# Layer 0 of a four-layer graph network: one wide first product on VectorE, and the destination's rows gathered from DRAM by GpSimd instead of selected by a one-hot product on TensorE

## The reference, cut to what matters

```
msg_s, msg_v = table_src[src] + table_dst[dst]        # 64 scalars, 32 vectors; tables = normed rows @ weights
w1 = rbf @ W_rbf                                      # 224 weights an edge, from 16 features
m1_s, m1_v = cg_tp(msg_s, msg_v, y0, y1, w1)          # first product
a = leaky(m1_s @ W_alpha) . alpha_dot                 # 4 logits an edge
alpha = softmax of a over the edges of one dst
val_s, val_v = m1 @ Ws_val, Wv_val, gated by sigmoids
m2_s, m2_v = cg_tp(val_s, val_v, y0, y1, w2)          # second product
agg[dst] += alpha * (m2 @ W_vlin)                     # 4 heads of 40

cg_tp(s, v, y0, y1, w): scalars  w_ss*s*y0, w_vv0*(v.y1)/sqrt3
                        vectors  w_sv*s*y1, w_vs*v*y0, w_vv1*cross(v, y1)/sqrt2
```

## Time and profile before

| | |
|---|---|
| median of 3 runs | 12166.53 us |
| the profiled execution, its own time | 12098.74 us |
| its span, first to last instruction | 12096.9 us |
| busy: PE, DVE, ACT, POOL | 9397.7, 9136.3, 7003.3, 6367.4 us |
| granted clock of TensorE, mean | 0.897 |
| layer 0's loop over pairs | about 1590 to 6550 us of the span |

### The profile page before, as it was taken

One profiled execution on the slowest core, in us unless ns is written; L12 is line 12 of the kernel. 1 busy time (PEld: TensorE's weight loads), 2 busy tenths in 40 slices (PEclk: granted clock), 3 DMA queues, 4 the chain that ended last, 5 costly groups with the idle time before them and its releaser, 6 DMA issues. The chain is left out here.

```text
span 12096.9 us, 245491 instructions
## 1 busy us (share of the span) xinstructions
PE 9397.7 (78%) x46500; PEld 6592.8 (55%) x46501; DVE 9136.3 (76%) x32454; ACT 7003.3 (58%) x26255; POOL 6367.4 (53%) x9502
## 2 busy tenths in 40 slices
PE   4421188888888888888888788887788888788887
PEld 1211177777777777777777344445433335444445
DVE  6702078888888888888887899995565555899996
ACT  0000067777777777777776555553566666676764
POOL 0677646666666666666542455551355553455551
PEclk9855589999999999999998999996799999999997
DMA  6433211111111111111111343333222223343333
GB/s 262 53 66 70 64 31 31 30 30 30 30 31 30 31 30 30 31 30 31 27 17 38 82 87 86 87 85 46 43 53 52 52 52 54 84 87 85 86 85 60
DMA packets 1798441, 691.91 MB, mean 57 GB/s; under 512 B 1586190, under 2 KB 1677258, under 8 KB 1798346
## 3 DMA queue, kind: packets, MB, share of 16 engines
q0 software_dynamic: 219136, 411.56, 14.6%
q1 hardware_dynamic: 1572154, 275.26, 13.5%
q10 hardware_dynamic: 7056, 4.02, 0.1%
HBM read 514.24 MB, written 171.77 MB: 57 GB/s over the span
## 5 line engine op out<-in xcount | busy, mean ns | idle before, releaser
L963 POOL DMA_INDIRECT shared<-table,rec x2640 | 2560.4, 970 | 2508.8 <-issue 1058.4
L1045 PE MATMUL bank<-tp,oh 128*128 128x480 f32 (+1 forms) x5280 | 2407.3, 552 | 6.3 <-DVE tp L1122 4.6
L997 ACT ACTIVATE tp<-tp,rec 128x64 f32<-128x64 f32 x7920 | 2030.3, 335 | 234.1 <-DVE tp L1093 153.2
L1037 PE MATMUL bank<-w_fc,hT 128*128 128x448 f32 x2640 | 1368.5, 601 | 701.5 <-ACT hT L981 447.9
L1680 ACT ACTIVATE shared<-bank 128x512 f32<-128x512 f32 x1760 | 973.6, 595 | 961.9 <-PE bank L1755 955.1
L1045 PEld LDWEIGHTS bank<-tp,oh 128*128 128x128 f32 x5280 | 921.0, 195 | 856.8 <-issue 843.5
L1755 PE MATMUL bank<-ident,tp 128*128 128x128 f32 x7040 | 1054.0, 299 | 265.5 <-ACT tp L813 218.2
L1093 DVE TENSOR_TENSOR tp<-bank,shared 128x256 f32<-128x256 f32 x1320 | 560.2, 424 | 924.3 <-PE bank L1045 613.4
L782 POOL DMA_INDIRECT rec_dst<-ACC x784 | 813.5, 1038 | 602.5 <-issue 571.9
L1755 PEld LDWEIGHTS bank<-ident,tp 128*128 128x128 f32 x7040 | 889.9, 154 | 303.3 <-ACT tp L813 253.6
L1644 POOL DMA_INDIRECT gat<-table,rec x880 | 866.7, 985 | 277.0 <-issue 190.7
(11 more groups left out here) (248 smaller groups left out, 22541.0 us busy)
## 6 DMA issues: line engine op xcount, KB each, us to landing
shared<-table,rec POOLq DMA_INDIRECT x2640
rec_dst<-tp SPq DMA_DIRECT2D x44, 900.0 KB, 23.6
ACC<-in_attrs SPq DMA_DIRECT2D x56, 623.0 KB
rec_src<-tp SPq DMA_DIRECT2D x44, 730.0 KB, 19.9
efr<-rec_src SPq DMA_DIRECT2D x440, 64.0 KB
efr<-rec_dst SPq DMA_DIRECT2D x440, 64.0 KB
ACC<-in_attrs SPq DMA_DIRECT2D x196, 130.0 KB
rec<-rec_dst SPq DMA_DIRECT2D x1320, 10.0 KB
```

What stands on the lines that cost most here:

```text
L963: nc.gpsimd.indirect_dma_start(out=gatx[:, u, g, 0:L.row], out_offset=None, in_=tables[L.n][:, :], in_offset=IOff(ap=rec[:, u, g, L.idx:L. ...
L997: done = nc.scalar.activation(t[:, g, lo:lo + 64], t[:, g, 0:64], ACT.Copy, scale=rec[:, u, g, L.y + k:L.y + k + 1])
L1037: nc.tensor.matmul(pW[u % 2][:, 0:448], hT[:, u % 2, :], fc2[:, :], start=True, stop=True)\
L1045: done = nc.tensor.matmul(pS[u % 2][:, 0:TW], oh[:, u, g, :], tp[:, u % 2, g, 64:64 + TW], start=g == 0, stop=g == G - 1)
```

## The change

The destination's rows are stored to a DRAM table of their own, `table_d`, in the node work at the start (49 more DMAs of 80 KB on ACT's queue), and in the loop POOL gathers them by destination into `gat_d`: two more indirect DMAs a pair. The two matmuls of L1816 and PE's register load go. The record gets one more integer (90 to 91 floats), the destination. The first product becomes the wide form of `edge_loop`: ACT scales 96 of each group's weight columns by y0 in PSUM (two instructions), DVE makes the product, POOL no longer takes part. `message` becomes two instructions, with the first vector's column block written twice. Further: the write of the new maximum to `M` is moved from `maxima` to behind `weigh` (`held`); `gates` becomes one instruction for both groups; `weigh` becomes one instruction of 328 columns, since `pH` gets a column of ones for each head; DVE keeps one of its two block numbers in three steps of four. ACT makes the scalar part of the first product ahead of its copies of stage a, not behind them.

```diff
             def rows_out(b):
...
+                if b >= 1:
+                    dst_rows_out(b - 1)
+            def dst_rows_out(b):
+                ac.wait_ge(first_td_kept.h, first_td_kept.at(b + 1))
+                ac.dma_start(table_d[b * P:b * P + P, :], first_TD[:, b, :]).then_inc(first_dst_stored.h, 16)
...
POOL     gather(a):
+                            nc.gpsimd.indirect_dma_start(
+                                out=gat_d[:, s4, g, :], out_offset=None, in_=table_d[:, :],
+                                in_offset=IOff(ap=rec[:, s4, g, 2:3].bitcast(i32), axis=0))
...
POOL     step:
-                        if b:
-                            part(*b, msg[:, b[1] % 2], msg_ready, tp1_ready, 0, pooled1)
                         if a:
                             gather(*a)
                         if c:
-                            part(*c, vsv[:, c[1] % 2], gated, tp2_ready, 1, pooled2)
+                            part(*c)
...
ACT      step:
+                        if b:
+                            ac.wait_ge(sv1_ready.h, sv1_ready.done(*b))
+                            product_scalar(*b, tp[:, 0, :, 0:64], tp[:, 0, :, 64:544], L).then_inc(axes1.h, 1)
                         if a: (copies of efT and ohT)
-                        if b:
-                            ac.wait_ge(sv1_ready.h, sv1_ready.done(*b))
-                            product_scalar(*b, t_sv, 0, L).then_inc(axes1.h, 1)
...
                             product_scalar(*c, ...)
+                        if a:
+                            ac.wait_ge(w_ready.h, w_ready.done(*a))
+                            for g in range(G):
+                                y0w = pW[:, 224 * g + 64:224 * g + 160]
+                                last = nc.scalar.activation(y0w, y0w, ACT.Copy, scale=rec[:, a[1] % 4, g, L.y0:L.y0 + 1])
+                            last.then_inc(w_scaled.h, 1)
...
PE       step:
                         if a:
-                            row = block_of(pe, *a)
                             pe.wait_ge(copied.h, copied.done(*a))
-                            pe.wait_ge(msg_ready.h, msg_ready.free(*a, 1))
-                            for g in range(G):
-                                last = nc.tensor.matmul(pB[:, F * g:F * g + F], ohT[:, s4, g, :],
-                                                        flat(TD[:, row, :]), start=True, stop=True)
-                            last.then_inc(dst_ready.h, 1)
...
DVE      message:
-                        nc.vector.tensor_tensor(msg[:, u % 2], gat[:, u % 4], pB[:, 0:320]...)
+                        nc.vector.tensor_tensor(rows[:, u % 2, :, 0:F], gat[:, u % 4], gat_d[:, u % 4], ALU.add)
+                        nc.vector.tensor_tensor(rows[:, u % 2, :, F:F + 64], gat[:, u % 4, :, 64:128],
+                                                gat_d[:, u % 4, :, 64:128], ALU.add).then_inc(msg_ready.h, 1)
DVE      first product:
+                    def weighted_scalars(i, u):
+                        ve.wait_ge(msg_ready.h, msg_ready.done(i, u))
+                        ve.wait_ge(w_scaled.h, w_scaled.done(i, u))
+                        ve.wait_ge(t1.h, t1.free(i, u, 1))
+                        nc.vector.tensor_tensor(tp[:, 0, :, 0:128] (both parts), w[:, :, 0:128], rows 0:64 twice, ALU.mult)
+                    def first_product(i, u):
+                        for g in range(G): nc.vector.tensor_tensor(vy0[:, g], (3x3x32), (3x3 axes), ALU.mult)
+                        nc.vector.tensor_tensor(tv[:, :, :, 64:96], v, along(128), ALU.mult)
+                        nc.vector.reduce_sum(t_sum[:, :, :], vy0[:, :, 0]..., AX.X)
+                        nc.vector.tensor_tensor(cross0[:, :, :, :], vy0[:, :, 1], vy0[:, :, 2], ALU.subtract)
+                        nc.vector.tensor_tensor(t[:, :, 128:160], t_sum[:, :, :], w[:, :, 160:192], ALU.mult)
+                        nc.vector.tensor_tensor(tv[:, :, :, 96:128], cross0[:, :, :, :], along(192), ALU.mult)
...
DVE      step:
+                            block_e = last_block[0] if last_block else block_of(ve, *e)
                         if b:
                             message(*b)
                         if d:
                             highest(*d)
                             maxima(*d, block_d)
                         if a:
                             one_hot(*a)
+                        if b:
+                            weighted_scalars(*b)
                         if d:
                             distances(*d)
                         if b:
+                            first_product(*b)
...
                             weigh(*d)
+                            held(*d, block_d)
```

234 lines of the change are left out of this document (115 added, 119 removed).

## The result

The kernel after takes 13,653.71 us (median of 4 runs, 13,614.36 to 13,721.11) against 12,161.1 us for the kernel before (4 runs, 12,148.45 to 12,169.12): ratio 1.123, interval 1.119 to 1.128. It is 12% slower. The forecast was 11,886 us, and the slowest rival stood at 12,355.

A forecast was written before the change was run, and what follows sets the result against it. DVE was taken to set layer 0's pace, with PE close behind. 440 pairs x 0.65 us = 286 us, less 5 for node work, gave 281 off 12,166.5: 11,886 us; 8-in-10 range 11,790 to 12,070.

The forecast's parts named there:

- the sentence under PE: Layer 0, PE's hand-overs: its 0.13 us of lateness should fall; that gain and new lateness elsewhere were taken to cancel, 0.
- The step before it: Layer 0, POOL: two gathers cost 2.64 us, work becomes 9.10 us in a 10.6 us step; gathers slow DVE by 0.
- DVE's sum: Layer 0, DVE's chain: the terms add to a gain of 0.67 us a pair, 0.65 used over 440 pairs.
- The first product: Layer 0, DVE: the wide form takes 2.29 us instead of 2.56, a gain of 0.27 us a pair.
- `mdiff` to the one-hot: Layer 0, DVE's maxima: moving the copy behind `weigh` and losing a wait gains 0.23 us a pair (0.15 to 0.28).
- `weigh`: Layer 0, DVE: one instruction of 328 columns at 0.42 us replaces three at 0.54, a gain of 0.12 us.
- The contention that was taken as unchanged: Layer 0: the second product keeps its POOL part and its slowing of DVE, as L836's 447 ns for 285.
- Rival 1: Layer 0: new waits in hand-overs, such as logits' transposes, give back 0.3 us a pair; 12,018 us, chance 0.2.
- Rival 3: Layer 0: indirect DMAs hold up DVE's two-SBUF-operand instructions, 0.85 us a pair; 12,255 us, slower, chance 0.04.
- The rule that was weighed against the sum there: Layer 0: two-SBUF-input DVE instructions and SBUF-reading GpSimd ones exclude each other; gathers' slowing of DVE still taken as 0.
- Rival 4: Layer 0: POOL becomes the bound if gathers take longer, at 2.0 us each 12,355 us; slower, chance 0.04.
- Rival 5: Layer 0: PE's clock falls because PE has less to do, and the gain is gone; 12,159 us, chance 0.05.

The follow-up runs named there:

- e10: The kernel after, unchanged, run again on the second chip, where no updates are held: 11,252.76 us, 0.962 of the kernel before.
- e3: The kernel after with POOL waiting for the new maximum ahead of its gathers, destination's rows by one-hot product again, two gathers for four: 11,792.8 us, 0.968.
- e18: e3 repeated on a fourth chip: 0.965 of the kernel before.
- e19: e3 with POOL waiting for the turned mask instead of the new maximum, so gathers start earlier; fourth chip: 0.965 of the kernel before.
- e6: The kernel before with two copies of 560 elements a pair added on POOL, into a buffer nobody reads; second chip: 1.073.
- e7: The kernel before with two further gathers a pair, of 64-byte rows instead of 640, into a buffer nobody reads; second chip: 1.006.
- e4: The kernel before with two further gathers of full rows a pair beside its two, into a buffer nobody reads; first chip: 12,853.23 us, 1.054.
- e17: e7 repeated on a third chip, one with held updates: 1.048 of the kernel before.

## Why the prediction was wrong

**The step that failed** is the sentence under PE: "I take nothing for it and nothing for new lateness of other hand-overs". The hand-overs from PE to DVE and ACT became 1.16 us late in the mean, 3 us a turn on DVE directly and 4.9 with what follows. The step before it had the facts and didn't use them: POOL's gathers were costed on POOL (right) and asked whether they slow DVE's instructions (right, they don't), but not what they lie beside once `part(b)` is gone, nor that they would join the scatters. The trace of before holds a small sign of it in layer 0: one PE line, L1805, held 0.20 us in the mean, the one line that ends 2.6 us into the gathers. The prediction left the times of the updates out altogether.

**That the holding is the cause** is shown by pairs of the same kernel with and without it: after 1.12 and 0.962; the one-hot version without a wait 1.032 and 0.962; two more gathers 1.054 and 1.006, with short rows 1.048 and 1.006. In all four pairs the held time goes with the loss. The chip changes with it in each of them, so the pairs by themselves can't tell the holding from something else in which the chips differ; that DVE's idle time makes up the whole difference in a turn (4.90 of 4.88 us), most of it in waits for updates that are late, is what puts the loss on the holding. That a group's length sets the hold is read from five kernels' traces and was not tested by itself, and part of the held updates doesn't fit it, as said above. What makes a chip hold, or not, stays open. So does whether it belongs to a chip at all: the second chip was seen in two rounds, the others in one.

**DVE's sum was right, and too small.** The first product, in the slow kernel, goes from 4006.33 to 4008.69 with one other instruction in it (0.07 us), so 2.29 as forecast. The message is 0.40 and then its second addition; `mdiff` to the one-hot is 0.09 us in e10 and the copy 0.10 later, so 0.30 gained for 0.23; `weigh` is 0.41 for 0.42. Busy time in e10 is 9.37 us a turn against 9.95, 0.58 less. Its idle time fell too, from 1.32 to 0.87 us, which the sum had at nothing; 0.26 of that is the issue time ahead of the message, 77.4 us over 177 turns before and 34.6 over 195 in e10. A turn of 10.24 us for the forecast's 10.6 is the result. On the second chip the change gave 443 us, for 281 forecast: 11,253 us of 11,696.

**The contention that was taken as unchanged is about unchanged.** In e10 POOL's part of the second product meets two of DVE's instructions, L1856 and L1857, at 430 and 431 ns in the mean; in the slow kernel, where it mostly runs before them, they take 294 and 292. That is 0.14 us a turn each:

```profile
L1857 DVE TENSOR_TENSOR tp<-rec,vsv x440: 278/430/435, 1472.5 to 5975.0; 128x128 f32<-128x128 f32 x147
```

Before, it met two as well, of which the prediction saw one, L836 (443 ns in the mean for 287). The other is L835, 365 ns for 215:

```profile
L835 DVE TENSOR_TENSOR t_cr<-vsv,rec x373: 209/414/422, 1699.7 to 5891.1; 128x64 f32<-128x64 f32 x187
L835 DVE TENSOR_TENSOR t_cr<-msg,rec x373: 212/215/219, 1706.6 to 5898.0; 128x64 f32<-128x64 f32 x187
```

So some 0.3 us a turn before and after, and the sum holds.

**The rivals.** Rival 1 (new waits) had the right kind and named the right place first, the transposes of the logits, but as a chain that is too long, at 0.3 us. Rival 3 (indirect DMAs hold up DVE) is refuted. In e10 about half of the nine products run beside a gather, and they take 452 ns beside one and away from it. In the slow kernel hardly any do (10 of 556), but its message's second addition, L1811, mostly does: 283 ns beside a gather, 284 without. The nine products first in the slow kernel, then in e10:

```profile
L1833 DVE TENSOR_TENSOR ACC<-ACC,rec x880: 446/451/505, 1591.0 to 8091.4; 128x288 f32<-128x288 f32 x176
```

```profile
L1833 DVE TENSOR_TENSOR ACC<-ACC,rec x880: 450/452/488, 1461.8 to 5960.5; 128x288 f32<-128x288 f32 x176
```

The rule that was weighed against the sum there would bear out the third rival only if a gather were such a reader, and by these times it isn't one. Rival 4 (POOL as the bound) is refuted by POOL's 5.9 us of waiting and a pitch of 1.25 to 1.3 us between gathers. Rival 5 (the clock) happened, but as a consequence: PE waits first, 2.4 us a turn ahead of L1751, and the clock is 0.72; in e10, with the same work, it is 0.96. How much of the 4.9 us the clock has was not separated; the wait for L1773, 0.9 us, is its clearest part.

**The version to use** is e3, which is e18: the wide product with the new order, the destination's rows by the one-hot product, the source gathers behind the new maximum. It beats the kernel before by 3.2 and 3.5% on two chips with held updates, and the kernel after by 14% if their ratios are compared (0.968 and 1.123, which are from different runs of the kernel before). On the chip without them it was not run; its relative without the wait takes 0.962 there, the same as the kernel after.

## What to carry to other kernels

A GpSimd step that goes away is also a spacer that goes away: list what its neighbours then lie beside on the other engines, and whether they join into a longer row. Ahead of indirect gathers ask which of TensorE's results is needed during them and within a microsecond after; where the order is free, put the gathers beside results whose reader comes late, with a wait if need be. And a result that one chip gives can be another chip's opposite: before a ratio is used to accept or reject a change, look at whether its mechanism (here, the updates' lateness) is there in the trace.

## What the runs showed of the hardware

- On three of four chips an update of PE that falls into a group of indirect gathers comes late, for the most part only when the group is over, up to 3.1 us late in the mean for one line (L1743, after). The recorded ends of PE show none of it; "remote" in the waits, or an idle time ahead of the reader, does. DVE's instructions keep their durations, and their updates come 0.01 us behind their ends in the same traces.
- Update records of PE can be missing: 583 of 2,325 in e19, 204 of 2,130 in the kernel before; on the second chip 66 of 2,148 in e10 and none of 1,827 in e6.
- The scatters alone hold little: in the kernel before, 8 of the 169 updates in the microsecond in which they end were held over 0.3 us, and the mean is 0.05 us.
- It isn't the bytes of the two further gathers: with 64-byte rows L1810 is held 2.46 us, with 640-byte rows 2.49.
- The kernel before is 4% faster on the chip without held updates (11,700 us for 12,193), and not in layer 0, where its own updates are hardly held. Its first reduce of layer 0 lies at 1602 us in the profile above and at 1475 us in e7, and from the last one to the end it takes 5,550 and 5,284 us. In those stages PE's updates are held as well: among those that can be matched to their instruction, 0.29 us in the mean between 7000 and 8000 us and 0.7 in the node work between 500 and 1000 us, for 0.01 in both in e7. Whether that makes the whole difference was not tested.
- Two copies of 560 columns on POOL cost more (1.9 us a turn) than two more gathers with held updates (1.4 us, e4 and e17), all against the 11.27 us of the kernel before.
